# Spherical conversion moved from a stage of its own into the kNN stage, and row statistics moved from VectorE to ScalarE

## What is computed

```python
# layer 0: chunked cross attention (8 heads, chunks of 64) of ctx, projected, plus x, then a norm over T
out = _chunk_attn(q, k, v, masks, ...) + x                  # (32, 128, 1024), called y below
x1 = (out - mean(out, 2)) * rsqrt(var(out, 2) + 1e-5)
# layer 1: for each of the 1024 points the 30 nearest of ctx's first three channels ...
rel = pts[bidx, idx] - pts[:, :, None, :]
sxy2 = xr * xr + yr * yr
rho = sqrt(max(sxy2 + zr * zr, TINY))
theta, phi = arctan2(zr, sqrt(sxy2)), arctan2(yr, xr)
feat = concatenate([sph, sph - mean(sph)])                  # sph = rho, theta, phi
h = three layers of feat @ W.T with batch norm over everything and leaky relu
att = softmax(h, axis=-1)                                   # over the 30 neighbours
result = x1 + sum over neighbours of att * x1[neighbour]
```

## Time and profile before

| what | value |
|---|---|
| median of 3 runs | 5831.81 us (5822.1 to 5831.84) |
| profiled execution | 5827.65 us, its span 5825.8 us |
| busy in the span | VectorE 91%, TensorE 79%, ScalarE 67%, GpSimd 43% |
| mean granted clock of TensorE | 0.901 |

### The profile page before, as it was taken

One profiled execution on the slowest core, in us unless ns is written; L12 is line 12 of the kernel. 1 busy time (PEld: TensorE's weight loads), 2 busy tenths in 40 slices (PEclk: granted clock), 3 DMA queues, 4 the chain that ended last, 5 costly groups with the idle time before them and its releaser, 6 DMA issues. The chain is left out here.

```text
span 5825.8 us, 167066 instructions
## 1 busy us (share of the span) xinstructions
PE 4613.9 (79%) x62610; PEld 2686.8 (46%) x63182; DVE 5315.0 (91%) x7589; ACT 3901.7 (67%) x9258; POOL 2479.7 (43%) x3044
## 2 busy tenths in 40 slices
PE   6888888888888888888888888830185799999999
PEld 2444444444444444444444444420032666666666
DVE  7999999999999999999999999947898988888887
ACT  3777777777777777777777777753434666766766
POOL 3566666666667666666666666630000000000000
PEclk7999999999999999999999999965598899999999
DMA  0010001000100001000100010000000000000000
GB/s 30 16 31 17 16 17 31 16 17 17 31 17 16 17 20 27 17 16 17 31 16 17 17 31 16 9 5 0 0 0 0 30 26 30 26 32 30 26 30 26
DMA packets 135652, 114.61 MB, mean 20 GB/s; under 512 B 105328, under 2 KB 105840, under 8 KB 134640
## 3 DMA queue, kind: packets, MB, share of 16 engines
q1 hardware_dynamic: 134768, 102.73, 6.0%
HBM read 69.16 MB, written 33.55 MB: 18 GB/s over the span
## 5 line engine op out<-in xcount | busy, mean ns | idle before, releaser
L559 ACT ACTIVATE ohT<-oh_ps 128x512 bf16<-128x512 f32 x1920 | 1149.4, 614 | 439.9 <-PE oh_ps L453 314.2
L802 DVE MAX8 vals<-pd_sb 128x8 f32<-128x1024 f32 x1024 | 1203.7, 1214 | 138.5 <-ACT pd_sb L559 121.5
L807 DVE FIND_INDEX8 idx<-vals,pd_sb 128x8 uint16<-128x1024 f32 x1024 | 1245.1, 1219 | 0.0
L474 PEld LDWEIGHTS g_ps<-tparts,ohT 128*128 128x128 bf16 x23040 | 847.5, 97 | 343.8 <-issue 81.3
L809 DVE MATCH_REPLACE8 pd_sb<-vals,pd_sb 128x1024 f32<-128x1024 f32 x768 | 928.7, 1209 | 0.0
L474 PE MATMUL g_ps<-tparts,ohT 128*128 128x24 bf16 x23040 | 866.8, 174 | 68.3 <-issue 31.2
L1881 PEld LDWEIGHTS e_a_ps<-planes,e_oh 120*128 120x128 bf16 x24576 | 687.9, 97 | 292.8 <-issue 212.2
L1652 ACT COPY e_at<-e_a_ps 128x512 f32<-128x512 f32 x512 | 542.5, 1059 | 350.5 <-PE e_a_ps L1881 344.6
L1881 PE MATMUL e_a_ps<-planes,e_oh 120*128 120x32 bf16 x24576 | 702.5, 178 | 75.9 <-DVE e_oh L1809 46.8
L378 PE MATMUL pd_ps<-ctx_s 128*128 128x512 f32 x1024 | 639.2, 709 | 68.3 <-ACT pd_sb L559 65.8
L453 PE MATMUL oh_ps<-bitsT,code 128*128 128x512 bf16 x1348 | 549.8, 412 | 162.8 <-ACT bitsT L716 120.8
(11 more groups left out here) (234 smaller groups left out, 6654.0 us busy)
## 6 DMA issues: line engine op xcount, KB each, us to landing
ctx_s<-in_ctx SPq DMA_DIRECT2D x32, 512.0 KB, 4.6
maskb<-in_mask_Bx1x_ff SPq DMA_DIRECT2D x32, 512.0 KB, 6.3
x_s<-in_x SPq DMA_DIRECT2D x32, 512.0 KB, 5.5
y_spill<-y_s SPq DMA_DIRECT2D x32, 512.0 KB, 3.0
e_y<-y_spill SPq DMA_DIRECT2D x32, 512.0 KB, 3.9
out<-e_o SPq DMA_DIRECT2D x64, 256.0 KB, 2.0
table<-in_ctx SPq DMA_DIRECT2D x96, 4.0 KB, 5.9
pd_sb<-in_shape_constants SPq DMA_DIRECT2D x1, 1024.0 KB, 5.2
```

Source lines behind the costliest of these rows:

```text
L474: m = nc.tensor.matmul(found_ps[gi % 2][:, k % GK, t, :], ohT[:, k % OHR, bass.ts(t, P)], tparts[:, par, part, :], start=(part == 0), stop ...
L559: return nc.scalar.activation(dst, src, func, scale=scale, bias=bias)
L802: nc.vector.max(vals[:, i, :], pd_sb[:, (t + i) % RING, :]).then_inc(topk_step, 1)
L807: found = nc.vector.max_index(idx16[:, par, t + i, 8 * r:8 * r + 8], vals[:, i, :], work)
```

## The change

In stage A each batch's relative positions are converted two to three batches after their gather. ScalarE does Arctan of the ratios and Square after tile 2, two Sqrt and an Abs after tile 4; GpSimd does 23 steps on 240 (two of them on 480) columns, each waiting for the one before; VectorE takes one reciprocal. The angles are computed by half-angle ratios, so that stage B needs no conversion and phi and theta change places (the weights' rows are built accordingly). The sums of y and of its squares are accumulated by ScalarE passes, after tile 3 for half 1 of the batch before and after tile 6 for half 0; the load of x waits for them, because they write their waste into `x_s`. Stage E makes mean and variance from the sums in six small VectorE steps. Some constants no longer stay in SBUF; iota is loaded again in stage E. Four batches instead of two are written out ahead of the loop.

```diff
...
@@ stage A, SP @@
-                sp.dma_start(x_s[:], x[b]).then_inc(x_landed, 16)
                 if not last:
                     load_mask(b + 1, 1 - par)
                 if not (isinstance(b, int) and b < 2):
                     gate(sp, g_done, (b - 1) * NG, sp_gates)
                 load_table(b, par)
+                if not first:
+                    gate(sp, row_summed, b * 2, sp_gates)
+                sp.dma_start(x_s[:], x[b]).then_inc(x_landed, 16)
...
@@ stage A, ScalarE, emit @@
+                    if t == 2:
+                        if there(b - 3):
+                            angles(b - 3)
+                        if there(b - 2):
+                            rel_squares(b - 2)
+                    if t == 4 and there(b - 2):
+                        roots(b - 2)
+                    if t == 3 and not first:
+                        row_sums(b - 1, 1)
+                    if t == 6:
+                        row_sums(b, 0)
...
+            def rel_squares(d):
+                gate(act, g_done, (d + 1) * NG, act_gates)
+                if not (isinstance(d, int) and d == 0):
+                    gate(act, sph_step, (d - 1) * SPH_STEPS + SPH_RATIOS, act_gates)
+                nc.scalar.activation(rel2[:], sph(d), ACT.Square).then_inc(rel_squared, 1)
+            def roots(d):
+                rel = sph(d)
+                gate(act, sph_step, d * SPH_STEPS + SPH_SIGNS, act_gates)
+                nc.scalar.activation(rel2[:, 2, :], rel[:, 0, :], ACT.Abs).then_inc(x_kept, 1)
+                nc.scalar.activation(rel2[:, 0, :], rel2[:, 0, :], ACT.Sqrt)
+                gate(act, x_kept, d + 1, act_gates)
+                nc.scalar.activation(rel[:, 0, :], rel2[:, 1, :], ACT.Sqrt).then_inc(roots_taken, 1)
+            def angles(d):
+                gate(act, sph_step, d * SPH_STEPS + SPH_RATIOS, act_gates)
+                ratios = sph(d)[:, 1:3, :]
+                nc.scalar.activation(ratios, ratios, ACT.Arctan).then_inc(angles_taken, 1)
...
+            def row_sums(b, h):
+                gate(act, y_ready, b * 2 + h + 1, act_gates)
+                half, spent = y_s[:, h, :], x_s[:, bass.ts(h, HALF)]
+                one = bass.ds(b, 1)
+                nc.scalar.activation(spent, half, ACT.Identity, accum_out=row_acc[:, h, one]).then_inc(sum_step, 1)
+                if h == 0:
+                    gate(act, sum_step, b * 3 + 1, act_gates)
+                    move(row_acc[:, 4, one], row_acc[:, 0, one], scale=-1.0 / HALF).then_inc(sum_step, 1)
+                gate(act, sum_step, b * 3 + 2 + h, act_gates)
+                nc.scalar.activation(spent, half, ACT.Square, bias=row_acc[:, 4, one],
+                                     accum_out=row_acc[:, 2 + h, one]).then_inc(row_summed, 1)
...
+            row_sums(B - 1, 1)
+            angles(B - 3)
+            rel_squares(B - 2)
+            bits(tail)
+            gather(B - 1, 0, 0, K)
+            roots(B - 2)
+            bits(tail)
+            gather(B - 1, 1, 0, K)
+            angles(B - 2)
+            rel_squares(B - 1)
+            roots(B - 1)
+            angles(B - 1)
...
@@ stage A, VectorE @@
-            def row_stats(b, h):
-                dve.wait_ge(y_ready, b * 2 + h + 1)
-                nc.vector.bn_stats(bnst[:, h, :], y_s[:, h, :]).then_inc(bn_step, 1)
-                if h == 1:
-                    if not (isinstance(b, int) and b == 0):
-                        dve.wait_ge(mv_kept, b)
-                    gate(dve, bn_step, b * 2 + 2, dve_gates)
-                    nc.vector.bn_aggr(mv[:], bnst[:].rearrange("p h s -> p (h s)")).then_inc(mv_ready, 1)
...
+                        if t == 6 and r == 1 and there(b - 2):
+                            denoms(b - 2)
                         if t == 2 and r == 2 and not first:
                             digits(b - 1, 1 - par, 1)
-                            row_stats(b - 1, 1)
                         if t == 6 and r == 2:
                             digits(b, par, 0)
-                            row_stats(b, 0)
+            def denoms(d):
+                dve.wait_ge(sph_step, d * SPH_STEPS + SPH_DENOMS)
+                nc.vector.reciprocal(rel2[:, 1, :], rel2[:, 1, :]).then_inc(denoms_turned, 1)
...
@@ stage A, GpSimd @@
+            def sph_signs(d):
+                rel = sph(d)
+                steps = Steps(d * SPH_STEPS, sph_step, True)
+                gate(pool, rel_squared, d + 1, pool_gates)
+                steps(nc.gpsimd.tensor_tensor(rel2[:, 0, :], rel2[:, 0, :], rel2[:, 1, :], ALU.add))
+                steps(nc.gpsimd.tensor_tensor(rel2[:, 1, :], rel2[:, 0, :], rel2[:, 2, :], ALU.add))
+                steps(nc.gpsimd.tensor_scalar(solid[:], rel2[:, 0:2, :], TINY, None, ALU.is_ge))
+                steps(nc.gpsimd.tensor_scalar(rel2[:, 0, :], rel2[:, 0, :], TINY, None, ALU.max))
+                steps(nc.gpsimd.tensor_tensor(rel2[:, 1, :], rel2[:, 0, :], rel2[:, 2, :], ALU.add))
+                steps(nc.gpsimd.tensor_tensor(rel2[:, 2, :], rel[:, 0, :], solid[:, 0, :], ALU.mult))
+                steps(nc.gpsimd.tensor_tensor(rel[:, 1, :], rel[:, 1, :], solid[:, 0, :], ALU.mult))
+                steps(nc.gpsimd.tensor_tensor(rel[:, 2, :], rel[:, 2, :], solid[:, 1, :], ALU.mult))
+                steps(nc.gpsimd.tensor_scalar(rel2[:, 2, :], rel2[:, 2, :], 0.0, -2.0, ALU.is_lt, ALU.mult))
+                steps(nc.gpsimd.tensor_scalar(rel2[:, 2, :], rel2[:, 2, :], 1.0, None, ALU.add))
+                steps(nc.gpsimd.tensor_tensor(turn[:], rel[:, 1, :], rel2[:, 2, :], ALU.mult))
+                steps(nc.gpsimd.tensor_tensor(rel[:, 1, :], rel[:, 1, :], rel2[:, 2, :], ALU.mult))
+                steps(nc.gpsimd.tensor_scalar(turn[:], turn[:].bitcast(I32), 0, PI, ALU.is_lt, ALU.mult))
+                steps(nc.gpsimd.tensor_scalar(turn[:], turn[:], PI / 2, None, ALU.subtract))
+                steps(nc.gpsimd.tensor_scalar(rel2[:, 2, :], rel2[:, 2, :], -0.5, 0.5, ALU.mult, ALU.add))
+                steps(nc.gpsimd.tensor_tensor(turn[:], turn[:], rel2[:, 2, :], ALU.mult))
+                assert steps.n == SPH_SIGNS
+            def sph_denoms(d):
+                rel = sph(d)
+                steps = Steps(d * SPH_STEPS + SPH_SIGNS, sph_step, True)
+                gate(pool, roots_taken, d + 1, pool_gates)
+                steps(nc.gpsimd.tensor_tensor(rel2[:, 2, :], rel2[:, 2, :], rel2[:, 0, :], ALU.add))
+                steps(nc.gpsimd.tensor_tensor(rel2[:, 0, :], rel2[:, 0, :], rel[:, 0, :], ALU.add))
+                steps(nc.gpsimd.tensor_tensor(rel[:, 2, :], rel[:, 2, :], rel2[:, 2, :], ALU.mult))
+                steps(nc.gpsimd.tensor_tensor(rel[:, 1, :], rel[:, 1, :], rel2[:, 0, :], ALU.mult))
+                steps(nc.gpsimd.tensor_tensor(rel2[:, 1, :], rel2[:, 0, :], rel2[:, 2, :], ALU.mult))
+                assert steps.n == SPH_DENOMS - SPH_SIGNS
+            def sph_ratios(d):
+                both = sph(d)[:, 1:3, :]
+                steps = Steps(d * SPH_STEPS + SPH_DENOMS, sph_step, True)
+                gate(pool, denoms_turned, d + 1, pool_gates)
+                steps(nc.gpsimd.tensor_tensor(both, both, rel2[:, 1:2, :].to_broadcast([P, 2, BCOLS]), ALU.mult))
+            def sph_turn(d):
+                phi = sph(d)[:, 1, :]
+                steps = Steps(d * SPH_STEPS + SPH_RATIOS, sph_step, True)
+                gate(pool, angles_taken, d + 1, pool_gates)
+                steps(nc.gpsimd.tensor_tensor(phi, phi, turn[:], ALU.add))
...
+                    if t == 0 and there(b - 3):
+                        sph_ratios(b - 3)
+                    if t == 3:
+                        if there(b - 3):
+                            sph_turn(b - 3)
+                        if there(b - 2):
+                            sph_signs(b - 2)
+                    if t == 5 and there(b - 2):
+                        sph_denoms(b - 2)
...
+            sph_ratios(B - 3)
+            convert(B - 1, 1)
+            sph_turn(B - 3)
             gather(B - 1, 1, 0, range(GROUPS), steps)
-            convert(B - 1, 1)
+            sph_signs(B - 2)
+            sph_denoms(B - 2)
+            sph_ratios(B - 2)
             gather(B - 1, 1, 1, range(GROUPS), steps)
-            pool.wait_ge(mv_ready, B)
-            nc.gpsimd.tensor_copy(stats_all[:, B - 1, :], mv[:]).then_inc(mv_kept, 1)
-            pool.wait_ge(g_done, B * NG)
-            pool.wait_ge(mv_kept, B)
+            sph_turn(B - 2)
+            sph_signs(B - 1)
+            sph_denoms(B - 1)
+            sph_ratios(B - 1)
+            sph_turn(B - 1)
+            pool.wait_ge(sph_step, B * SPH_STEPS)
...
@@ stage B @@
-                with dve.Fori(0, CH) as c:
-                    base, aa = c * V_PER + 1, c * A_PER
...
-                do(v.tensor_tensor(S["mat"][:], S["ab"][:], inner(S["rs"][:], 3), ALU.subtract))
+                do(v.tensor_tensor(S["mat"][:, :, 0], S["ab"][:, :, 0], S["rs"][:], ALU.subtract))
```

(49 more changed lines are left out.)

137 lines of the change are left out of this document (43 added, 94 removed).

## The result

The changed kernel took 5854.8 us (median of 5 runs, 5850.16 to 5862.16) against 5831.81 before, a ratio of 1.0044 with a 95% interval of 1.0033 to 1.0055: slower by 23 us. The forecast was 5844, 12 us slower, with a chance of 0.48 for slower and 0.39 for faster. The profiled execution took 5862.16 us, 34.5 more than the profiled one of before and at the upper end of its own runs.

The account below looks back on a forecast made before the run. VectorE was taken to pace stage A, ScalarE with TensorE its stretch from tile 3's exponents to tile 7's distances. 5827.65 - 327.2 + 283.2 + 54 + 2 = 5839.6, with 4.2 for the median 5844 us; range 5735 to 5955.

Parts of the forecast that it names:

- The block that goes away: Stage B's conversion to spherical coordinates, with TensorE and GpSimd idle, goes away as a whole: 327.2 us less.
- ScalarE's chain: Stage A, exponents of tile 3 to distances of tile 7: ScalarE's added passes and table loads cost 7.3 us a batch.
- VectorE: Stage A: an added reciprocal of 1.6 us, less 0.3 for statistics dropped, costs 1.3 us a batch net.
- Tail: End of stage A, where nothing covers the conversion: 54 us longer (42 to 65), about 119 us in all.
- Loop: Stage A's batches: 9.6 us more each, over 29.5 batches +283 us.
- the clock: Stage A: new pauses lower TensorE's granted clock, costing 1.0 us a batch, between 0 and 3.
- The drain of 1.38 us: Rule against the forecast: each table switch in stage A costs 2.66 us, making the sum 163 us higher, 6007.
- so nothing is added, but it is close: Stage A: GpSimd's added 21.7 us a batch stay hidden, the keys of tile 6 by 0.8 us.
- Small: Tiny VectorE steps in stage B, the iota load and six steps in stage E: +2 us.
- TensorE's lead covers ScalarE's absence: Rival, stage A: half of 7.3 stays, 6 us a batch, 5738 us; chance 0.27 for below 8.
- GpSimd becomes the bound: Rival, stage A: sign steps 0.3 us longer add 5.8 us a batch, 6015 us; chance 0.15 for above 12.

Follow-up runs that it names:

- e_few_steps: The changed kernel with 11 of GpSimd's 16 sign steps a batch left out, so that the signs of the angles are missing: 5775.4 us.
- e_no_switch: The changed kernel with Arctan made an Identity and both Sqrt an Exp, so without the four table loads a batch: 5843.82 us.
- e_both: The changed kernel without the four table loads a batch and without 11 of GpSimd's 16 sign steps: 5590.0 us.
- e_sums_only: The kernel before with only the row sums of y moved to ScalarE and stage E's six small steps, conversion still in stage B: 5859.82 us.
- e_sums_back: The changed kernel with the row statistics of y back on VectorE, the conversion left as changed: 5823.49 us.
- r_split2_sums: r_split1 with Sqrt and Abs after tile 2, and row sums on ScalarE after tiles 2 and 6: 5861.2 us.
- r_split1: The changed kernel with row statistics on VectorE, conversion in other tiles: 9 sign steps in tile 7, 7 in tile 0, Sqrt and Abs after tile 1: 5747.99 us.

## Why the forecast was right, and where it was not

The sum came out within 11 us of the median: +23 us for a forecast of +12. The block, ScalarE's chain, VectorE and the tail are right by their mechanism. The loop's number is in part luck: a wait that was put at nothing came to about 1.3 us a batch, and the terms beside it were together about 1 us too large. Point by point:

- **The block that goes away**, 327.2 us: as read.
- **ScalarE's chain**, 7.3 us a batch and 1.0 for the clock. The forecast had the exponents of tile 5 7.3 us later; by the mean of 27 batches they start 11.4 us after their maximum, 4.6 before: +6.9. Those of tile 3 start 2.2 us after theirs (forecast 2.8). With the keys in time (e_few_steps) the loop grows by 7.8 us a batch in all, of which 0.2 is VectorE's own (reciprocal 1.64, statistics -1.72, L848 and L852 0.31) and 7.5 are its waits. So ScalarE's and TensorE's line alone costs about 7.5, against the 8.3 of the sum. The 1.0 for the clock is not shown apart: the granted clock fell from 0.93 to 0.90, but no run separates what that cost. The reading that these waits lie at one place of each batch holds for 29 of the 42 before (300 to 3800 us); 13 lie at tile 3. The 94.5 us of the earlier trace rows leave out two waits at the start of the stage; with them it is 121.5 us in 45. The loads are 1.28 each and are on the path. The drain of 1.38 us that the Trainium skill adds (ScalarE: Activation LUTs, What ACT_TABLE_LOAD costs) is not in the records, and 1.5 us a load in the time leaves no room for 2.66.
- **GpSimd, "so nothing is added, but it is close"**: this is the step that failed. The 16 steps on signs took what was worked out (2110.52 to 2125.98 in one batch, 15.5 us against 15.2). From the maximum of tile 3 (1973.13) to the keys of tile 6 it took 43.4 us, against 33.5 before (2004.79 less 1971.3), so the keys moved by 9.9 instead of 9.3. On the other side the scores could have started when the exponents of tile 5 had ended (2017.63) and 0.14 us had passed, as is usual between the two: 44.6 us after that maximum, not 45.5, as ScalarE's line was 6.5 us late here and not 7.3. The keys ended at 2018.38, so 0.8 us of margin became -0.6. A margin that is the difference of two estimates of 9 and 7 us is none. By VectorE's waits with and without the 11 steps the cost is 1.3 us a batch; by the lateness of the keys alone it is 1.1.
- **VectorE**, +1.3: 1.64 - 1.72 + 1.18 = +1.1, right by cancelling. I had counted only part of the statistics as a gain and not seen that L848 and L852 would get slower; without the 11 steps (e_few_steps) 0.3 of the 1.18 are left.
- **Loop**: +10.0 a batch for 9.6, 11 us of the 295. The shares are not those of the forecast: about 7.5 for the line of ScalarE and TensorE (7.3 and 1.0 were forecast), 1.1 for VectorE (1.3), 1.3 for the keys (nothing). e_no_switch shows why the shares matter: a forecast of that one edit by my chain alone was wrong by some 140 us.
- **Tail**: 120.2 us for 119. The terms written down for it add up to 55.8, not 54; the measured growth is 55.2. Each term by itself was not measured.
- **Small**: +1.8 to the root of stage E, as put. The rest of stage E took 1312.5 us instead of 1302.9. In the experiments it took 1306.2 to 1316.3 us, also in those that kept its statistics as before (the span less the root's start; only one execution of each is profiled). This stays open.
- **The rivals.** "TensorE's lead covers ScalarE's absence" is refuted by e_both and e_few_steps, which differ in the loads alone: without them the loop is 1.7 us a batch longer than before, with them 7.8. "GpSimd becomes the bound" was true in part, at a price of about 1.3, not 5.8. What I treated as alternatives are two lines that both have to be shortened.

## What to carry to other kernels

Where two engines' lines meet within a microsecond, an edit to one is worth what the other leaves: here 9.5 and 63.9 us alone, 244 together. When an instruction waits for two things, its idle time is not the price of the later one: take the end of the later less the end of the earlier (here 31.9 us of 62.4). Before placing work on a "free" engine, take the room of each of its deliveries (start of the user less end of the delivery), tile by tile, and cut the work into pieces that fit; the share of idle time (GpSimd was idle 36% of the loop) said nothing about a lump of 15 us. Moving 1.7 us of statistics off VectorE onto ScalarE as 3.6 us of passes was a loss each time it was tried: by 1.0 us a batch (e_sums_only), 1.4 (the changed kernel against e_sums_back) and 4.0 (r_split2_sums).

## What the runs showed of the hardware

Two VectorE instructions that nobody changed, L848 and L852, took 2 to 7 times as long in some batches (L848 0.29 us, or 1.1 or 2.0). One such case, VectorE and GpSimd in order of time, kernel after:

```profile
2296.91 2.06 DVE L844 TENSOR_TENSOR bits<-idx,bitval 128x896 uint16<-128x896 uint16 x1
2298.89 1.14 DVE L848 TENSOR_SCALAR hi<-idx 128x120 uint16<-128x120 uint16 x1
2300.06 1.26 DVE L852 TENSOR_TENSOR hi1h<-hi,hival 128x960 bf16<-128x960 uint16 x1
```

```profile
2296.59 1.90 POOL L1116 TENSOR_TENSOR kz<-kt,cst 128x1024 f32<-128x1024 f32 x1 [1.95 <-ACT kt L587]
2298.45 1.42 POOL L1092 TENSOR_TENSOR sS<-sS,rs 128x512 f32<-128x512 f32 x1
2299.82 0.99 POOL L1126 CAST bitsb<-bits 128x896 bf16<-128x896 uint16 x1
```

The keys end at 2298.49, and `bits` 0.48 us later; `hi`, 0.29 us otherwise, ends 0.16 us after GpSimd's next instruction; that one, 1.04 us otherwise, took 1.42. They take turns. Of the 53 records of L848 between 300 and 3700 us 17 are long, and in all 17 a GpSimd instruction was running at the start; in none of the 36 others was one; each of the 17 ended 0.16 us after that instruction. `bits` shows the same: in r_split1 28 of its 55 records have a GpSimd instruction running at their start and end 0.5 us after it, and the other 27 take 0.62 us. In the kernel before all 58 (L763, 1.12 to 1.24 us) are of the first kind, so one was held there already. This fits what the Trainium skill says of the port that the two share (SBUF — State Buffer, SBUF: two separate sides): "an exclusive lock, not a bandwidth split", held for the whole instruction. On L848 and L852 it cost 33 us in 28 batches here, all of it in tile 6, behind the wait, where VectorE paces; before, no record of L767 was long, and in e_few_steps 6 of 54. No experiment removed it alone.
